# Self attention's gating at once, its output normalised in PSUM, and GpSimd's context steps behind the key mask product

## What is computed

```
def _L0_ffn_ref(x, W_gate, W_qkv):
    H, hd = (N_HEAD, HEAD_DIM)                       # 16 heads of 16
    gating = jax.nn.softmax(x @ W_gate.T, axis=-1)
    idx = jnp.argmax(gating, axis=-1)
    indicator = jax.nn.one_hot(idx, H, dtype=gating.dtype)
    top1_val = jnp.max(gating, axis=-1, keepdims=True)
    gating_top1 = indicator * top1_val
    q, k, v = jnp.split(x @ W_qkv.T, 3, axis=-1)
    k_shared = jnp.einsum('bth,bthd->btd', indicator, k.reshape(Bb, Tt, H, hd))
    v_shared = jnp.einsum('bth,bthd->btd', gating_top1, v.reshape(Bb, Tt, H, hd))
    att = jnp.einsum('bhqd,bkd->bhqk', q, k_shared) * (1.0 / math.sqrt(hd))
    att = softmax(where(causal, att, -inf))
    y = jnp.einsum('bhqk,bkd->bhqd', att, v_shared)
...
x = x + _L0_xattn_ref(...)
x = x + _L0_ffn_ref(_layernorm(x, axis=-1), L0_ffn_W_gate, L0_ffn_W_qkv)
x = x + _L1_xattn_ref(...)
...
```

## Time and profile before

| | |
|---|---|
| median of 3 timed runs | 805.93 us (804.97 to 806.3) |
| span of the profiled execution, first to last instruction | 799.9 us |
| median of the timed runs less this span | 6.0 us |
| PE busy | 634.7 us (79%) |
| DVE busy | 504.4 us (63%) |
| ACT, POOL busy | 318.4 us (40%), 241.9 us (30%) |

### The profile page before, as it was taken

How to read it: one execution, slowest core, us unless ns; L and a number is a source line. 1 busy time by engine, 2 the same in 40 slices (tenths; PEclk the granted TensorE clock), 3 DMA queues, 4 the chain that set the end, 5 groups by cost and what they waited for, 6 DMA issues and landing times.

```text
span 799.9 us, 11194 instructions
## 1 busy us (share of the span) xinstructions
PE 634.7 (79%) x3782; PEld 400.0 (50%) x3799; DVE 504.4 (63%) x1079; ACT 318.4 (40%) x549; POOL 241.9 (30%) x247
## 2 busy tenths in 40 slices
PE   1651878895985269999886998877999999999990
PEld 1341434552663115566444666544666666666660
DVE  6998987886788999889667676963222222222223
ACT  4910432333566327887744566501111111111110
POOL 3212162446850189760322312002111111111100
PEclk9675898998998559999977999999999999999996
DMA  7000402020002543571215002980000000000005
GB/s 264 0 0 17 155 1 63 5 66 0 2 1 58 113 113 87 158 171 63 97 37 239 37 2 105 431 345 27 13 27 27 26 26 26 26 26 26 20 14 171
DMA packets 32318, 61.72 MB, mean 77 GB/s; under 512 B 6232, under 2 KB 26712, under 8 KB 29944
## 3 DMA queue, kind: packets, MB, share of 16 engines
q1 hardware_dynamic: 24480, 48.93, 19.2%
q10 hardware_dynamic: 5632, 6.29, 2.2%
q0 software_dynamic: 2160, 5.90, 2.1%
HBM read 47.22 MB, written 13.50 MB: 76 GB/s over the span
## 4 chain that ended last, share of the span: by engine, by line
PE 46%; DVE 24%; issue 4%; ACT 3%; POOL 2%; DMA 1%; DVEq 0%; POOLq 0%; SPq 0%; ACTq 0%
PE bank L1902 17%; PE bank L1923 8%; PE bank L1480 4%; DVE region L1208 4%; PE bank L1121 2%; PE bank L1913 2%; PE bank L1500 2%; PE bank L1105 2%; DVE XN L362 2%; PE bank L1081 2%; DVE wide L1197 1%; DVE region L763 1%; DVE region L760 1%; PE bank L2043 1%; PE bank L563 1%
## 5 line engine op out<-in xcount | busy, mean ns | idle before, releaser
L1902 PE MATMUL bank<-region,wide 128*128 x368 | 142.3, 540 | 1.6 <-DVE etab L1761 1.6
L1781 DVE TENSOR_TENSOR wide<-wide,bank 128x448 f32<-128x448 f32 x46 | 28.5, 621 | 119.9 <-ACT wide L1829 119.9
L1902 PEld LDWEIGHTS bank<-region,wide 128*128 128x128 f32 x368 | 68.3, 191 | 61.5 <-issue 61.4
L1208 DVE TENSOR_REDUCE region<-bank 128x2 f32<-128x512 f32 x128 | 80.2, 681 | 6.7 <-PE bank L1081 6.1
L1679 POOL DMA_INDIRECT choice_results<-wide,to_row x23 | 22.7, 987 | 182.9 <-DVE wide L1794 182.9
L1923 PE MATMUL bank<-region,XN 128*128 x322 | 73.4, 380 | 1.2 <-DVE wide L1794 1.2
L1144 ACT ACTIVATE region<-bank 128x1024 f32<-128x1024 f32 x64 | 62.8, 1024 | 15.6 <-PE bank L1105 15.5
L1829 ACT ACTIVATE wide<-bank 128x448 f32<-128x448 f32 x46 | 24.9, 543 | 106.2 <-PE bank L1902 106.2
L1923 PEld LDWEIGHTS bank<-region,XN 128*128 128x128 f32 x322 | 59.7, 191 | 9.2 <-issue 2.1
L1081 PE MATMUL bank<-region 128*128 128x256 bf16 x256 | 51.7, 303 | 9.0 <-DVE region L1208 6.1
L376 POOL TENSOR_TENSOR rstd<-vareps,half_neg 128x4 f32<-128x4 f32 x16 | 18.3, 1146 | 121.0 <-DVE vareps L372 121.0
(11 more groups left out here) (310 smaller groups left out, 1253.9 us busy)
## 6 DMA issues: line engine op xcount, KB each, us to landing
region<-in_L_ffn_experts_dram SPq DMA_DIRECT2D x8, 2688.0 KB, 15.8
region<-ctx_parts SPq DMA_DIRECT2D x24, 192.0 KB
region<-norm_parts SPq DMA_DIRECT2D x24, 192.0 KB
channel_values<-wide ACTq DMA_DIRECT2D x8, 512.0 KB, 3.5
ctx_parts<-region SPq DMA_DIRECT2D x40, 64.0 KB, 2.0
region<-in_L_ffn_w_gate_up_dram SPq DMA_DIRECT2D x4, 512.0 KB, 6.1
wide<-channel_values SPq DMA_DIRECT2D x16, 128.0 KB, 2.5
norm_parts<-region SPq DMA_DIRECT2D x24, 64.0 KB, 3.4
```

Source lines behind the costliest of these rows:

```text
L1208: e.tensor_reduce(nmax[i % 2][:, at_:at_ + KC], score_bank("scores", n).rearrange("p (c n) -> p c n", c=KC), AX.X, ALU.max, negate=True).t ...
L1781: e.tensor_tensor(HB8[par][:, cols], silu8[:, cols], bank[hf][:, 512:512 + I8 // 2], ALU.mult)\
L1902: last = e.matmul(bank[hf][:, 512 * gu:512 * gu + hw], xbT[par][:, P * c:P * c + P], region[:, bass.ds(off + (2 * gu + c) * I8 + hw * hf, ...
```

## The change

Three things in stage 0. The logits of all eight tiles are made ahead of the loop (`gate_logits`, 64 columns of one bank for each half of the tokens), and DVE works out all marks at once (`gates`, five instructions over 128 elements) and all reciprocals at once (`gate_weights`), with one exponential on ACT (`gate_exponents`); `select` keeps a product over 512 elements, the sum over heads, and the scaling. The attention output is normalised in place in PSUM and added to X from there, without the tile OA. GpSimd makes the context steps directly behind kbd and ahead of the next krep. DVE's six chunk sums all stand behind select(0).

```
@@ pool_attention
                     if t >= 1:
                         e.wait_ge(s_att["key_T_ready"], t)
                         kbd(t - 1)
+                        for p in ((0,), (1, 2), (3,), (4,), (5,), (6, 7), (8,), (9,))[t - 1]:
+                            pool_context_part(e, ch, p // 5, p % 5)
                     if t < NT:
                         e.wait_ge(s_att["kv_selected"], t + 1)
                         if t >= 1:
                             e.wait_ge(s_att["key_T_in_psum"], t)
                         e.tensor_copy(krep, ...).then_inc(s_att["key_repeated"], 1)
-                    if t >= 1:
-                        for p in ((0,), (1, 2), (3,), (4,), (5,), (6, 7), (8,), (9,))[t - 1]:
-                            pool_context_part(e, ch, p // 5, p % 5)
@@ pe_attention
+            def gate_logits(hf):
+                for i in range(4 * hf, 4 * hf + 4):
+                    for c in range(KC):
+                        last = e.matmul(ps(4, H * i, H * i + H), XT[:, c, P * i:P * i + P], wgT[:, c, :],
+                                        start=(c == 0), stop=(c == KC - 1))
+                last.then_inc(s_att["logits_made"], 1)
+
             def key_value(i):
                 if i >= 2:
                     e.wait_ge(s_att["kv_selected"], i - 1)
-                    e.wait_ge(s_att["key_T_ready"], i - 1)
-                if i >= 4:
-                    e.wait_ge(s_att["out_normalised"], NT * s + i - 3)
...
                 for c in range(KC):
-                    e.matmul(ps(4 + i % 2, 288, 288 + H), XT[:, c, P * i:P * i + P], wgT[:, c, :],
-                             start=(c == 0), stop=(c == KC - 1))
-                for c in range(KC):
                     last = e.matmul(ps(6 + i % 2), XT[:, c, P * i:P * i + P], wqkvT[:, c, D:3 * D], ...)
             def key_T(i):
                 e.wait_ge(s_att["key_repeated"], i + 1)
+                if i == 0:
+                    e.wait_ge(s_att["gates_read"], 1)
                 if i >= 4:
-                    e.wait_ge(s_att["out_normalised"], NT * s + i - 3)
+                    e.wait_ge(x_done, NT + i - 3)
...
                 key_value(0)
+                gate_logits(0)
                 for hf in range(2):
                     e.wait_ge(s_turned, TURN["att0"] + KC * (hf + 1))
+                    if hf == 1:
+                        gate_logits(1)
                     project_half(wqkvT, 0, XT, hf, KC * hf, s_att["q_in_psum"])
@@ act_attention
                 for c in range(TW // TCH):
-                    if c == 2:
-                        gate_sum(0)
                     if c == 4:
                         leave_half(QT, 0, 0, s_att["q_in_psum"], s_att["q_ready"])
                     act_ternary_cast(e, c)
+                    if c == 1:
+                        gate_exponents()
...
-                if s == 0 and 1 <= t < NT:
-                    gate_sum(t)
@@ vec_attention
+            def gates():
+                lg = ps(4, 0, NT * H).rearrange("p (t h) -> p t h", h=H)
+                e.wait_ge(s_att["logits_made"], 2)
+                e.wait_ge(s_att["consts"], 4)
+                ch.link(e.tensor_reduce(gate_max, lg, AX.X, ALU.max))
+                e.tensor_tensor(logit, lg, gate_max..., ALU.subtract).then_inc(s_att["gates_read"], 1)
+                e.wait_ge(s_att["gates_read"], 1)
+                ch.link(e.scalar_tensor_tensor(first_max, logit, 0.0, revh..., ALU.is_ge, ALU.mult))
+                ch.link(e.tensor_reduce(gate_pick, first_max, AX.X, ALU.max))
+                ch.link(e.tensor_tensor(gate_hot, first_max, gate_pick..., ALU.is_equal))
+
+            def gate_weights():
+                e.wait_ge(s_att["gates_raised"], 1)
+                ch.link(e.tensor_reduce(gate_sum, gate_exp, AX.X, ALU.add))
+                ch.link(e.reciprocal(gate_rec, gate_sum))
+
             def select(i):
                 e.wait_ge(s_att["kv_made"], i + 1)
+                ind = gate_hot[:, i, :].unsqueeze(1).unsqueeze(3).broadcast_to([P, 2, H, HD])
+                ch.link(e.tensor_tensor(tmp..., ps(6 + i % 2)..., ind, ALU.mult))
                 if i == 0:
...
+                    gate_weights()
                 ch.link(e.tensor_reduce(SEL[:, i, :]..., tmp..., AX.X, ALU.add))
-                e.tensor_scalar(SEL[:, i, HD:2 * HD], SEL[:, i, HD:2 * HD], gate[:, 5, 2:3], None, ALU.mult)...
+                e.tensor_scalar(SEL[:, i, HD:2 * HD], SEL[:, i, HD:2 * HD], gate_rec[:, i:i + 1], None, ALU.mult)...
@@ normalise, s == 0
-                    dst = OA[:, i, :]
-                    e.tensor_tensor(dst..., out_, rec..., ALU.mult).then_inc(s_att["out_normalised"], 1)
-                    e.wait_ge(s_att["out_normalised"], i + 1)
-                    xi = X[:, D * i:D * i + D]
-                    e.tensor_tensor(xi, xi, dst, ALU.add).then_inc(x_done, 1)
+                    ch.link(e.tensor_tensor(out_, out_, rec..., ALU.mult))
+                    xi = X[:, D * i:D * i + D].rearrange("p (h d) -> p h d", d=HD)
+                    e.tensor_tensor(xi, xi, out_, ALU.add).then_inc(x_done, 1)
@@ loop of vec_attention
                 if s == 0 and t == 0:
                     vec_f8_weights(e, ch)
-                    for c in range(2):
-                        vec_ternary_sums(e, ch, c)
+                    gates()
                 if s == 0 and t < NT:
                     select(t)
                 if s == 0 and t == 0:
-                    for c in range(2, TW // TCH):
+                    for c in range(TW // TCH):
                         vec_ternary_sums(e, ch, c)
```

More of the change, by code:

```diff
@@ L176, in program @@
         SEL = carve(NT, 2 * HD)
-        OA = carve(NT, D)
+        logit = carve(NT, H)
+        first_max = carve(NT, H)
+        gate_exp = carve(NT, H)
+        gate_hot = carve(NT, H)
+        gate_max, gate_pick, gate_sum, gate_rec = (carve(NT) for _ in range(4))
         KBD = [[carve(HC, P) for _ in range(KC)] for _ in range(2)]
@@ L554, in values @@
                 if i >= 2:
-                    e.wait_ge(s_att["out_normalised"] if s == 0 else s_att["out_quantised"], i - 1)
+                    e.wait_ge(x_done if s == 0 else s_att["out_quantised"], i - 1 + (NT if s == 0 else 0))
                 if s == 0:
@@ L595, in pe_attention @@
                 if s == 1 and t == 2:
-                    e.wait_ge(s_att["out_normalised"], NT)
+                    e.wait_ge(x_done, 2 * NT)
                     quantised_T(1, 4)
@@ L623, in queries, with gate_exponents @@
                 leave_half(QT, hf, first, s_att["q_in_psum"], s_att["q_ready"], bqcol, base=4)
[L625 to L630, removed]
+            def gate_exponents():
+                e.wait_ge(s_att["gates_read"], 1)
+                e.activation(gate_exp.rearrange("p a b -> p (a b)"), logit.rearrange("p a b -> p (a b)"),
+                             ACT.Exp).then_inc(s_att["gates_raised"], 1)
             def key_T(i):
@@ L724, in quantise_norm @@
                         .then_inc(s_att["norm_quantised"], 1)
+            def gates():
[3 more added lines that the diff above has]
+                ch.link(e.tensor_reduce(gate_max, lg, AX.X, ALU.max))
+                e.tensor_tensor(logit, lg, gate_max.unsqueeze(2).broadcast_to([P, NT, H]), ALU.subtract)\
+                    .then_inc(s_att["gates_read"], 1)
+                e.wait_ge(s_att["gates_read"], 1)
+                ch.link(e.scalar_tensor_tensor(first_max, logit, 0.0, revh.unsqueeze(1).broadcast_to([P, NT, H]),
+                                               ALU.is_ge, ALU.mult))
+                ch.link(e.tensor_reduce(gate_pick, first_max, AX.X, ALU.max))
+                ch.link(e.tensor_tensor(gate_hot, first_max, gate_pick.unsqueeze(2).broadcast_to([P, NT, H]), ALU.is_equal))
@@ L730, in select @@
                 if i == 0:
[L731 to L738, removed]
@@ L739, in select @@
-                ch.link(e.tensor_tensor(gate[:, 1, :], gate[:, 0, :], revh, ALU.mult))
-                ch.link(e.tensor_reduce(gate[:, 5, 1:2], gate[:, 1, :], AX.X, ALU.max))
-                ch.link(e.tensor_scalar(gate[:, 2, :], gate[:, 1, :], gate[:, 5, 1:2], None, ALU.is_equal))
-                ind = gate[:, 2, :].unsqueeze(2).broadcast_to([P, H, HD])
-                for sv in range(2):
-                    last = e.tensor_tensor(tmp[:, D * sv:D * sv + D].rearrange("p (h d) -> p h d", d=HD),
-                                           ps(6 + i % 2, D * sv, D * sv + D).rearrange("p (h d) -> p h d", d=HD),
-                                           ind, ALU.mult)
@@ L747, in select @@
-                ch.link(last)
-                e.wait_ge(s_att["gate_sum_ready"], i + 1)
-                e.reciprocal(gate[:, 5, 2:3], gate[:, 5, 0:1])
+                    gate_weights()
                 ch.link(e.tensor_reduce(SEL[:, i, :].rearrange("p (s d) -> p s d", d=HD),
                                         tmp.rearrange("p (s h d) -> p s d h", h=H, d=HD), AX.X, ALU.add))
```

(5 more changed lines are left out.)

5 lines of the change are left out of this document (2 added, 3 removed).

## The result

The changed kernel takes **791.79 us** (791.54 to 794.42, 4 runs) beside 805.59 (804.97 to 806.3, 4 runs) for the kernel before: ratio 0.985 [0.981, 0.988], 13.8 us faster. Faster was forecast, but 799.9 in a range of 797.0 to 804.2: a gain of 6.0.

What follows compares the result with a forecast made beforehand. A dependency loop through several engines was taken to set the 9.35 us period. Start +9.0, selects 1 to 7 -13.2, last select -1.5, drain -1.8 and half clock +1.5 gave -6.0: 799.9 us, range 797.0 to 804.2.

Steps and rivals of the forecast that it cites:

- the base: Median 805.93 us against profiled span 799.9; their difference of 6.0 treated as unchanged, and the gain added to the median.
- the sum: The stage's terms for start, selects and drain give -7.5 us; half clock of +1.5 makes the total -6.0.
- Start, +9.0: Ahead of the loop DVE must wait for all logits, so select(1) starts at 106.8, not 97.77.
- Loop, 7.5: A late iteration's period falls from 9.35 us to 7.5, bound by PE, with selects of 2.0.
- Context steps: On GpSimd, two moved steps behind kbd(1) make krep(2) 1.6 us late; from select(3) on they cost nothing.
- Drain, 6.0: From the last select to the last shift: 6.0 us instead of 7.79, a gain of 1.8.
- Half clock in the start, +1.5: PE idles some 3.6 us behind scores(0), so 3.4 to 6.8 us at half clock follow, costing 1.5.
- Sum in PSUM, nothing: DVE's residual sum, with one input in PSUM, can't be blocked by GpSimd, but this gains nothing.
- the rival's 3.0: Residual sums still held up by GpSimd's context steps, 0.96 a time, four times: +3.0 us, total 802.9; chance 0.05.
- half clock in the tight loop: Rival: one more half-clock spell in the loop costs up to 4.2 us, total 802.8 to 804.1; chance 0.13.
- a start at half clock: Rival: clock rises only behind the second eight logit matmuls, +5.5 us, about 805.4, no measurable change; chance 0.11.

Runs made afterwards that it cites:

- e1: The kernel before, unchanged, run again for a second trace: 805.74 us, ratio 1.001.
- e6: The kernel before with five dummy matmuls ahead of the fourth and later transpositions, filling PE's loop pauses: 801.34 us, ratio 0.996 to the kernel before.
- e9: The changed kernel with seven dummy matmuls ahead of scores(0) and six ahead of key_T(1): 794.57 us, ratio 0.988 to the kernel before.
- e5: The changed kernel, unchanged, run again for a second trace: 793.68 us, ratio 0.989 to the kernel before.
- e3: The changed kernel with the normalised attention output through the SBUF tile again: 796.32 us, ratio 0.990 to the kernel before.
- e4: The changed kernel with all six chunk sums ahead of the gates and ACT's casts ahead of its exponential: 793.17 us, ratio 0.985 to the kernel before.
- e7: The changed kernel with four chunk sums ahead of the gates, two behind select(1), key_value(1) ahead of the loop, ACT's casts first: 790.56 us, ratio 0.982.
- e11: e9 with three pauses of cross attention also filled by dummy matmuls: 792.37 us, ratio 0.986 to the kernel before.
- e10: e6 with three pauses of cross attention also filled by dummy matmuls: 803.12 us, ratio 0.996 to the kernel before.
- e12: e7 with three pauses of cross attention filled by dummy matmuls: 786.90 us, ratio 0.979 to the kernel before.

## Why the prediction was off

**The step that failed is the base**: "I add what I find for the span to the median, and treat the 6.0 as unchanged." Only 1.8 of the 6.0 lies around the span. The other 4.2 was the difference between a lucky execution and an ordinary one, and e1 shows where most of it arises: one more stretch at half clock in the loop, with a span 2.9 longer. The forecast missed by 8.1 (799.9 for 791.79). Of that, 4.2 is this base. The change also gained 1.3 more between the two profiles than the sum had (7.3 for 6.0), and the profile after is of the longest of its four executions, 2.6 above their median.

The change takes away the pauses of 1.38 us beside which these stretches stand; no profile of a kernel with the new gating has one between select(3) and the stage's end, and e6, where only the pauses are filled, has none either. So an ordinary execution gains more than the one that the sum was made on. In numbers, at the stage's end: with no half clock from 87 us on, on either side, the change is worth 7.3 (e6 to e9); e1 to e5 is 13.1, e1 to the profile after 10.8. The 3.5 to 5.8 between is half clock: it costs e1 6.2 (to e6), and the changed kernel 0.4 to 2.7 (e9 to e5 and to after). Of the 13.8 measured this leaves 0.7 to 3 unexplained.

The clock ahead of the loop has a part in these numbers that the forecast didn't see. In the changed kernel the gates wait for PE, so it counts when the clock rises. In the microsecond from 85 on it was still at half in the profile after (first row) and at full in e9 (second row); key_value(0) took 3.62 and 2.64, and select(1) started at 105.58 and 104.21:

```profile
85.00:86.00 1.00, 1.00 (x2) 0.50 1.08 399
...
85.00:86.00 1.00, 1.00 (x12) 1.00 1.12 409
```

So some 1.2 of the 7.3 comes from the earlier rise in e9: 1.37 at select(1), less the 0.1 by which its stage starts earlier. In the kernel before key_value(0) took 3.16 to 3.75, and select(1), which stands behind the chunk sums, started at 97.4 to 97.8 throughout; no run has the clock rise before 85.9 there.

The other steps, by their own numbers:

- **Start, +9.0**: +7.8. Gates, select(0) and the six sums came within 0.2 of the forecast. The tail took 1.16 (104.42 to 105.58) instead of 2.17, as no mask product of GpSimd's runs beside it now: its first instruction took 1.18 before and 0.21 now (rows below). In e5 and e9 the start costs 6.8 and 6.4, as the clock rises earlier there.
- **Loop, 7.5**: 7.37, PE without idle time, selects of 2.0. Selects 1 to 7 took 42.40, with the half clock in them (forecast 41.9 + 1.5).
- **Context steps**: krep(2) 1.6 late was forecast; in e9 it is 1.1 late (112.55 for 111.41). In the profile after it is not seen, because key_value(2) at half clock had made select(2) late already. Krep(3) on is free, as forecast.
- **Drain, 6.0**: 6.2.
- **Half clock in the start, +1.5**: 1.3 in the profile after and nothing in e5, as select(1) to the stage's end takes 60.0 and 58.7 us, and 58.7 in e9 without half clock. PE's idle time ahead of key_T(1) was 1.90, not the 3.6 forecast. (Select(2) at 115.35 comes out as 115.0 by the forecast's own terms; nothing rests on it.) The Trainium skill's warning ("TensorE: Matmul & The Clock Gate", "HAM oscillation — how this bites in real kernels") agrees in that the stretch follows an idle time of PE's, 2.23 us, and is gone in e9, where PE's idle time there is filled but for 0.72, and that ahead of key_T(1) in part. Such a rule bears as much on the kernel before, whose pauses were shorter and more; I weighed it on one side alone.
- **Sum in PSUM, nothing**: right against the kernel before. Yet in the tight loop it holds off 1.9 us (e3), against the rival's 3.0, since two sums meet a long step there, not four.
- **Rivals**: half clock in the tight loop did not appear, nor did a start at half clock as long as the rival had it: the second sixteen logit matmuls took 1.85 in the profile after (and in e4 and e7), about the 4 x 0.44 that the forecast had for them.

The first instruction of the tail before, and the mask product that it ended with:

```profile
95.64 1.18 DVE L1263 TENSOR_SCALAR region<-region 128x96 bf16<-128x96 f32 x1
...
94.86 1.90 POOL L429 TENSOR_TENSOR region<-region,wide 128x1024 f32<-128x1024 f32 x1 [3.40 <-ACT region L636]
```

**What stays open**: what is gained in the stage is not always kept. The fills of e9 and e11 gave nothing over the changed kernel by their medians, and e10's gave nothing over e6. For e11 it may be that there was little to win: the two profiles of the changed kernel have no stretch at half clock between 190 and 240 us to be taken away. One profile (e10) shows the clock falling later instead. Which stretches the executions without a profile had was not shown; 1.3 of the 4.2 in the base lie between e1's profiled execution and the first median, and have no profile.

## What to carry to other kernels

Before adding a gain to a median, reconcile the profiled execution with it: if the difference exceeds what lies around the span, the profile is of an unusual execution, and a second profile, read for its stretches at half clock, can tell what the usual one has more of. A loop that leaves PE short pauses can pay twice, as here, in the pause and in the half clock beside it; a change that closes the pause is then worth more than its dependency chain says. Where a pause can't be closed, filling it with matmuls that compute nothing can pay (e6, e12), but look at the clock of every later stage, not only of the one that was filled.

## What the runs showed of the hardware beyond that

- Adding 25 matmuls that compute nothing made the kernel before 0.4% faster (e6; interval 0.2% to 0.6%).
- A small DVE instruction can be held up by GpSimd much like a large one: the scaling of 16 elements took 0.85 and ended with the context step beside it (e9, 109.25 + 2.13 = 111.38), and took 0.23 where no step ran.
- Stretches at half clock in this stage and in cross attention were 3.4, 6.8 or 10.2 us long, and the same start gave 10.2 in one execution and 3.4 in another (after, e5). A pause alone doesn't decide: of four profiles of the kernel before with the same pause of 2.12 us ahead of key_T(1), one has such a stretch behind it (e10).
